# Patch layers of a four-layer block: all ring copies on SP's queue, the first three rings one after the other

## What is computed

```
def patch_layer(x):                                  # x is the group-normed input, 192 channels
    t = einsum('bchw,oc->bohw', x, w_in)             # 1x1 projection
    tp = t.reshape(b, 192, 16, 8, 16, 8)             # patches of 8 x 8 pixels
    tp = irfft2(rfft2(tp) * fft_filter)              # a filter on each patch
    t = depthwise_conv_3x3(tp.reshape(b, 192, 128, 128), w_dw)     # 'SAME', across patch borders
    x1, x2 = t[:, :96], t[:, 96:]
    return einsum('bchw,oc->bohw', gelu(x1) * x2, w_out)
```

## Time and profile before

| | |
|---|---|
| median of three runs | 2428.84 us |
| the profiled execution | 2429.54 us |
| its span, from the first to the last instruction | 2427.7 us |
| mean granted TensorE clock | 0.958 |
| TensorE busy with matmuls | 2108.2 us, 87% |
| VectorE, ScalarE, POOL busy | 68%, 54%, 46% |
| layer 0's first and last convolution matmul | 214.1 and 285.7 us |
| layer 2's | 1965.3 and 2037.0 us |
| layer 3's | 2268.8 and 2342.0 us |

### The profile page before, as it was taken

One profiled execution on the slowest core, in us unless ns is written; L12 is line 12 of the kernel. 1 busy time (PEld: TensorE's weight loads), 2 busy tenths in 40 slices (PEclk: granted clock), 3 DMA queues, 4 the chain that ended last, 5 costly groups with the idle time before them and its releaser, 6 DMA issues. The chain is left out here.

```text
span 2427.7 us, 64964 instructions
## 1 busy us (share of the span) xinstructions
PE 2108.2 (87%) x23257; PEld 1587.5 (65%) x23384; DVE 1643.5 (68%) x3164; ACT 1301.4 (54%) x2727; POOL 1109.9 (46%) x1392
## 2 busy tenths in 40 slices
PE   0596997999899399999999999999987969879798
PEld 0473645888788277777777777777765646356463
DVE  5345585765565578888888888888874555735557
ACT  0254540085058567777777777777743545335453
POOL 0333250000000277777777887878763332533325
PEclk9998997999999699999999999999998989989899
DMA  9624595415723422222222222222216145961459
GB/s 218 184 82 74 117 331 150 127 26 194 222 31 127 146 52 62 59 58 58 58 58 58 58 58 58 58 58 59 60 45 185 35 88 150 308 183 42 88 139 320
DMA packets 305632, 272.30 MB, mean 112 GB/s; under 512 B 175966, under 2 KB 238846, under 8 KB 299210
## 3 DMA queue, kind: packets, MB, share of 16 engines
q1 hardware_dynamic: 294698, 256.00, 38.1%
q0 software_dynamic: 9280, 6.44, 2.4%
q10 hardware_dynamic: 1496, 7.63, 1.0%
HBM read 165.29 MB, written 81.46 MB: 102 GB/s over the span
## 5 line engine op out<-in xcount | busy, mean ns | idle before, releaser
L1701 DVE TENSOR_TENSOR l_scan_att<-l_scan_decay,l_scan_causal_scores 128x512 f32<-128x512 f32 x384 | 319.3, 832 | 64.4 <-ACT l_scan_decay L1670 64.1
L722 ACT COPY l_arena<-l_body_bank 128x384 f32<-128x384 f32 x192 | 142.0, 901 | 262.8 <-PE l_body_bank L590 262.8
L1664 ACT ACTIVATE l_scan_decay<-l_scan_cum 128x512 f32<-128x512 f32 x384 | 216.2, 597 | 33.1 <-PE l_scan_cum L1556 33.0
L1670 ACT ACTIVATE l_scan_decay<-l_scan_decay 128x512 f32<-128x512 f32 x384 | 227.8, 630 | 4.1
L1681 ACT ACTIVATE l_scan_yw<-l_scan_y_by_channel,l_scan_norm_b,l_scan_norm_w 128x128 f32<-128x128 f32 x384 | 148.0, 455 | 125.4 <-PE l_scan_y_by_channel L1618 118.4
L1603 PE MATMUL l_scan_gate_projected<-l_scan_xr,l_wf 97*128 97x128 f32 (+1 forms) x1536 | 205.3, 283 | 1.3 <-DVE l_scan_xo L1756 1.2
L652 PE MATMUL l_body_bank<-l_arena 100*64 100x128 f32 x2304 | 150.0, 286 | 59.8 <-DMA l_arena<-l_arena 59.8
L570 POOL TENSOR_TENSOR l_arena<-l_arena 96x512 f32<-96x512 f32 x96 | 122.7, 1278 | 168.8 <-ACT l_arena L788 162.8
L1521 POOL TENSOR_TENSOR l_scan_inter<-l_scan_inter,l_scan_xd 128x384 f32<-128x384 f32 x128 | 128.1, 1000 | 156.7 <-DVE l_scan_inter L1716 156.7
L1634 PE MATMUL l_scan_gate_projected<-l_scan_yz,l_scan_wo 128*96 128x128 f32 x1536 | 198.5, 279 | 1.1 <-DVE l_scan_yz L1733 1.1
L1634 PEld LDWEIGHTS l_scan_gate_projected<-l_scan_yz,l_scan_wo 128*96 128x96 f32 x1536 | 171.0, 163 | 40.0 <-issue 33.9
(11 more groups left out here) (191 smaller groups left out, 4814.9 us busy)
## 6 DMA issues: line engine op xcount, KB each, us to landing
l_scan_xc<-convolved_rows SPq DMA_DIRECT2D x128, 224.0 KB, 2.8
x_after<-l_arena SPq DMA_DIRECT2D x64, 384.0 KB, 4.9
l_arena<-x_after SPq DMA_DIRECT2D x64, 384.0 KB, 5.6
convolved_rows<-l_slots SPq DMA_DIRECT2D x48, 441.0 KB
l_conv_x_main<-x_after SPq DMA_DIRECT2D x64, 256.0 KB, 3.0
l_arena<-x_after SPq DMA_DIRECT2D x16, 1024.0 KB, 8.6
prepare_xt<-x SPq DMA_DIRECT2D x8, 1536.0 KB, 9.4
l_arena<-x SPq DMA_DIRECT2D x32, 384.0 KB, 5.5
```

The lines of the kernel that those rows point to most:

```text
L722: nc.scalar.copy(tA[:, b, :, j:j + 2].rearrange("p c q -> p q c"), bank[n % 4][:, 0:2 * C].rearrange("p (q c) -> p q c", q=2)).then_inc(t_ ...
L1664: nc.scalar.activation(decay[:, b % 2, 4 * g:4 * g + 4, :], cum[(b + g) % 2][:], ACT.Relu, scale=-1.0)\
L1670: nc.scalar.activation(group, group, ACT.Exp, scale=-1.0).then_inc(exp_done, 1)
L1701: nc.vector.tensor_tensor(att[:, b, 4 * g:4 * g + 4, :], decay[:, b % 2, 4 * g:4 * g + 4, :], causal[:, b % 2:b % 2 + 1, :].broadcast_to([ ...
```

## The change

The loop on POOL that issues the corner copies goes away, with the wait on `pads` before it. SP issues the six corner copies of a group right behind its four sides, on the same semaphores as before. And for groups 1 and 2 SP first waits until all ten copies of the group in front (in another strip) have landed. Groups 3 to 7 have no such wait. Everything else stays.

```
                 sp.wait_ge(pads, 4 * STRIPS)
                 for g in range(groups):
                     b = g % STRIPS
+                    if 1 <= g < STRIPS:
+                        sp.wait_ge(ringed[b - 1], 16 * RING_SIDES)
+                        sp.wait_ge(cornered[b - 1], 16 * (len(ring_strips()) - RING_SIDES))
                     sp.wait_ge(own_top, PIECES * (g + 1))
                     sp.wait_ge(own_low, PIECES * (g + 1))
                     for to, of, shift, _ in ring_strips()[:RING_SIDES]:
                         sp.dma_start(ring_pieces(strips[b], to, 0), ring_pieces(strips[b], of, shift)).then_inc(ringed[b], 16)
+                    for to, of, shift, _ in ring_strips()[RING_SIDES:]:
+                        sp.dma_start(ring_pieces(strips[b], to, 0), ring_pieces(strips[b], of, shift)).then_inc(cornered[b], 16)
                 sp.wait_ge(convolved, PIECES * (groups - 1))
...
-                pool.wait_ge(pads, 4 * STRIPS)
-                for g in range(groups):
-                    b = g % STRIPS
-                    pool.wait_ge(own_top, PIECES * (g + 1))
-                    pool.wait_ge(own_low, PIECES * (g + 1))
-                    for to, of, shift, _ in ring_strips()[RING_SIDES:]:
-                        nc.gpsimd.dma_start(ring_pieces(strips[b], to, 0), ring_pieces(strips[b], of, shift)).then_inc(cornered[b], 16)
                 for s in range(tiles):
```

## The result

The change makes the kernel slightly slower, by 0.4%. The median is 2437.68 us (10 runs, 2431.7 to 2445.19) against 2428.11 us (2423.51 to 2438.3) of the kernel before on the same chip: a ratio of 1.004, with a 95% interval of 1.002 to 1.0059. The profiled execution took 2437.33 us. 2384.0 us was forecast, so the 45.5 us that were to go away turned into 9.6 us more. The ring copies now have two lines: L521 issues the four sides and L523 the six corner copies, and the convolution's matmuls are L650.

What follows compares the result with a forecast made beforehand. The prediction blamed the convolution matmuls' 59.8 us of waits for ring copies. Earlier starts (38.9 us) plus the waits before groups 6 and 7 (6.65) made 45.5 us, taking 2429.5 to 2384.0 us, range 2371 to 2410.

Steps and rivals of the forecast that it cites:

- T: Time from a group's first ring issue to its whole ring's landing, claimed 10.5 us, range 9.2 to 13.9.
- Ten take 8.0 us: SP's issue time for a group's ten ring copies, claimed 8.0 us, below the 9.8 us a group lasts.
- 1.8 us per group: From group 4 on, SP's ring issues were to catch up on the convolution by 1.8 us per group.
- The cover of 1.3 us before group 7: Last layer: group 7's ring was to land at 2319.2, 1.3 us before convolve(7) wants it at 2320.5.
- the short waits: TensorE's six waits before groups 6 and 7 over three layers, 6.65 us, claimed to go away.
- The threshold: The waits before groups 1 and 2 were to cost nothing while a ring takes under 10.9 us.
- 9 us per us of T: Each us of ring time above 10.9 was to take 9 us from the gain.
- The start: First convolution matmul of each layer, claimed 12.4, 13.1 and 13.4 us earlier, 38.9 us in sum.
- A: Rival, chance 0.12: corner copies slow in themselves, starting behind the sides; ring takes 14.1 us, total gain 9 us, 2420.5 us.
- B: Rival, chance 0.06: serial rings become the bound, ring 2 landing after convolve(2)'s old start, T above 14.9 us; 2457 us.
- C: Rival, chance 0.03: the waits free nothing, convolve(0) starts as before and only the tail moves, 2422 to 2429 us.
- signs named for "wrong": Matmul waits before groups 1 and 2, SP issues of several us in a lone ring, or first wait staying 17 us.

Runs made afterwards that it cites:

- gates_only: Kernel before plus only the waits before groups 1 and 2, on SP and POOL, corner copies staying on POOL: 2423.32 us, ratio 0.9972.
- no_single_rows: Changed kernel without the four one-row copies, the convolution not reading rows 96 to 99: 2377.47 us, ratio 0.9797 to the kernel before.
- layout b: Changed kernel without its waits, pixels reordered into four eight-row sides, three reading rows four or nine apart, one reading eight neighbours: 2440.77 us, ratio 1.0052.
- rows8_layout_a: Changed kernel without its waits, pixels in plain order (row 8h + w), two of four eight-row sides reading neighbouring rows: 2503.21 us, ratio 1.0296.

## Why the prediction was wrong

**The step that failed is T, "T with all ten on SP": 10.5 us taken, 13.5 measured.** It was taken from group 3's ring of the kernel before, called "the nearest row" and read as 10.4 to 11 us. The row was read too long, and it was an exception. This window was at hand:

```profile
2290.00:2292.00 2.00, 2.00 (x32) 1.64 (x30) 1.58 (x3) 1.57 (x3) 0.00 (x0) 1.00 0.17 46
```

Its second half, 2291 to 2292 us, has a share of 0.01 and moves nothing, so that ring was through some 9.1 us after its first issue. Yet a ring that is alone in the very same arrangement, sides on SP and corners on POOL, takes 12.3 to 12.7 us in gates_only. So 1.8 to 2.2 of the 3 us were missing before anything moved to SP; why group 3's ring was that quick no run shows. The other 0.7 to 1.3 us are the single queue: from POOL the corners' slow transfer runs beside the sides' issues, and behind them in one queue it comes last. The sides take the first 6 us, and the corners' 210 KB then another 7.5. The two pairs of runs with and without one-row copies put 2.6 to 4.5 us of T on these four; of the two-row copies' part the runs only show that in no_single_rows, with nothing else left to move, 3 us go by at 41 GB/s:

```profile
2217.00:2220.00 3.00, 0.20 (x3) 0.00 (x0) 3.00 (x6) 2.50 (x5) 0.00 (x0) 0.81 0.12 41
```

**The cause is the partitions, not the queue.** The four one-row copies into rows 96 to 99 add 4.3 to 4.5 us to a ring that is alone, for 105 KB: some 24 to 25 GB/s and 1.1 us each, however they are cut, and as one copy hardly less; eight neighbouring rows as source give 62 to 64 GB/s where rows four apart give 200. The prediction left it open between "POOL's queue" and "copies that read and write one or two partitions", and then costed it as if it were the first. The Trainium skill has the rule: "SBUF — State Buffer", section "Door 1: The DMA port swizzle (why `[64,N]` ≈ `[32,N]`)", says that a partition's port is set by bits 4 to 2 and bit 6 of its number, so four neighbouring partitions, and the four 32 further on, share one of 16 ports of 27.2 GB/s. By that rule an estimate for a one-row copy is 26.9 thousand bytes / 27.2 GB/s = 1.0 us; rows 96 to 99 are one port, eight neighbours are two (54.4 GB/s), and rows 28 and 60, or 0 and 32, the sources of the two-row copies, are one as well. That makes 4.0 us for the four one-row copies, where the runs show 4.3 to 4.5 with the waits and 2.6 to 3.3 without, and 2.0 us for a two-row copy, which no run shows by itself; with one behind the other the six take 7.9 us by this estimate, and the windows show 7.5. For eight neighbours the runs show 62 to 64 GB/s in all, above the 54.4 of that rule, and the measurement decides. The rule stood against the change and was missed.

**"Ten take 8.0 us" failed with it.** The issues of the sides held (4 in 3.2 us), but in the last layer the six of the corners took 7.8 us in ring 0 and 6.3 to 7.2 later. The median of L521 was the kernel before's; the queue stretches the issues of slow copies, as this row of L523 shows (ns, min/median/max):

```profile
L523 SPq DMA_DIRECT2D l_arena<-l_arena x144: 547/914/2622, 193.8 to 2336.5; - x144
```

So SP needs 9.6 to 10.1 us per ring where a group of the convolution takes 9.8, and never catches up the "1.8 us per group". The cover of 1.3 us before group 7 was not there: its ring went out 2.9 us after its place, and the short waits grew instead of going away.

**The threshold held.** "The two waits cost nothing as long as T < 10.9": at T = 9.2 they cost nothing to be seen (2377.5 with, 2380.2 without), at 13.5 they cost 16.7 us, at 13.8 in layout b 10 us. By the forecast's own sum they hold convolve(2) until 3T instead of T + 21.9 us, which is 5.1 us a layer and 15 us in all at T = 13.5, close to the 16.7. (Its "9 us per us of T" is 6 for these waits and 3 for the later starts.)

**The start held in kind.** 38.9 us were counted, and 29.8 came: 10.1, 10.4 and 9.2, the three differences in T.

**T alone is half of the miss.** For T = 13.5 the forecast itself gives 2410 us, and 2437.68 came. From first issue to last matmul the three layers were to shrink by 45.5 us and grew by 8.0, 53.5 us apart. Of these, 9.1 us are the start. Another 29.5 us are waits behind it where none was forecast, 11.3 before groups 1 and 2 and 18.2 before groups 3 to 7. SP takes some 10 us for a ring and not 8, so the last ones are issued late, and in the last layer group 6 and 7 start 14.3 and 14.9 us behind their ring's first issue. The last 15 us are TensorE's own work: matmuls that took longer.

**The clock after a new stall was not in any sum.** 14.4 of those 15 us are in seven groups that begin after a wait of 1.9 to 4.0 us, and at their start the granted clock is 0.50 to 0.68. In the last layer it is 2.9 + 1.4 us, at 0.50, the level of 1.2 GHz, after TensorE had idled for 3.13 and 3.98 us; a wait of 1.93 us before group 6 cost nothing there.

**The rivals.** The mechanism is A's: the corner copies are slow in themselves and start behind the sides. Its price was not: A had T = 14.1 us, and its 9 us of gain are the lead that convolve(2) still has over the kernel before (2.4, 3.1 and 3.4 us), kept to the end. Measured from the first issue, convolve(2) starts 5.6, 6.0 and 5.2 us earlier than before (layers 0, 2 and 3), more than A left, and the last matmul ends 0.8, 4.3 and 3.0 us later. The lead is lost behind the start of group 2, by the clock and the late rings. The sign is B's, which had 0.06, though not its place: T stayed under B's 14.9 us. So A's mechanism came with B's sign by what neither of them counted. C fell: the waits, or the one queue, do free ring 0. The change as a whole is a sum of +17 from the waits and -7 from the one queue. Two of the signs named for "wrong" did come: waits before groups 1 and 2, and issues of 1.85 and 2.44 us in a ring that is alone.

What stays open: the two-row copies' own share of T, why group 3's ring took 9.1 us where a lone ring 0 takes 12.3 to 12.7, and why two pieces per row make the kernel slower. Not tried is a layout in which the corner pixels too lie in rows that don't neighbour each other, so that all copies would read and write spread rows.

## What to carry to other kernels

Before a copy inside the on-chip memory is costed by its bytes, look which partitions it reads and writes: a few neighbouring rows move at a fraction of the rate of rows four apart, and 22% of the bytes can be half of the time. Wait between transfers only when each transfer is shorter than the work that covers it; one queue in the right order gives the first transfer its priority for nothing. Don't take a price from a single row: the one ring of group 3 took 9.1 us, and rings in the same arrangement took 12.3 to 12.7. And a stall of 3 to 4 us costs more than its length here, since a group behind it took 12.7 us instead of 9.8.

## What was not expected of the hardware

- Copies into one of rows 96 to 99 move at some 24 to 26 GB/s in sum (105 KB add 4.3 to 4.5 us to a lone ring; with 4 pieces SP needs 4.21 us for four). Whether a row has 2, 4, 16 or the kernel's own pieces, T is 13.0 to 13.8 us.
- Eight neighbouring source rows: 62 to 64 GB/s at a busy share of 0.45 to 0.51, where rows four apart have 200 GB/s at 0.51. The share says nothing of the rate.
- SP's issue of a copy grows with what stands in the queue: 0.76 us in the median of the sides, up to 2.62 us for a corner copy, and 9.61 us for four in rows8_layout_a.
- How a row is cut changes not T but what follows: the eighth ring goes out 66.8 us after the first with 4 pieces, 70.0 with the kernel's own, and the medians are 2412.4, 2420.6 and 2435.0 us for 4, 16 and 2 pieces.
